# Attention outputs turned in 32x32 blocks by the vector engine instead of as whole tiles by the tensor engine

## The reference

```
q = heads([ctx, LN(x)] @ Wq)                      # 32 heads of 16
k, v = heads(LN(x) @ Wk), heads(LN(x) @ Wv)       # 8 heads, each for 4 query heads
sk, sv = heads(ctx @ Wsk), heads(ctx @ Wsv)
s = q @ [sk, k].T / 4 + slope[head] * (key - query), only where 0 <= query - key < 64
x1 = x + tanh(g0) * (softmax(s) @ [sv, v]) @ Wo
p = softmax(LN(x1) @ w_router); the 4 best of 128 experts, normalised
basis = silu(LN(x1) @ w_gate) * (LN(x1) @ w_up)   # 8 blocks of 256
out = x1 + tanh(g1) * ((sum of blocks by the experts' mix) @ w_down + shared expert)
```

## Time and profile before

| | |
|---|---|
| median of 3 runs | 991.57 us (988.68 to 991.63) |
| the profiled execution | 991.21 us, of which the span is 989.4 |
| PE busy | 923.0 us, 93% of the span |
| DVE busy | 569.0 us, 58% |
| ACT busy | 420.1 us, 42% |
| POOL busy | 370.4 us, 37% |
| mean granted PE clock | 0.984 of full speed |

### The profile page before, as it was taken

How to read it: one execution, slowest core, us unless ns; L and a number is a source line. 1 busy time by engine, 2 the same in 40 slices (tenths; PEclk the granted TensorE clock), 3 DMA queues, 4 the chain that set the end, 5 groups by cost and what they waited for, 6 DMA issues and landing times.

```text
span 989.4 us, 18083 instructions
## 1 busy us (share of the span) xinstructions
PE 923.0 (93%) x6936; PEld 793.9 (80%) x6936; DVE 569.0 (58%) x1135; ACT 420.1 (42%) x906; POOL 370.4 (37%) x401
## 2 busy tenths in 40 slices
PE   6779999999999999989998987899999999999998
PEld 6678989888898989977786775578888888888886
DVE  5356574756657474765122665836565565655657
ACT  5665453454444444464311432334444444344431
POOL 2020010100000010002000998445687887888841
PEclk9979999999999999999999998999999999999999
DMA  6585556665656555698000004461201201201026
GB/s 221 169 204 155 126 157 176 152 183 135 175 142 173 129 152 139 157 250 255 2 21 22 22 22 138 129 219 30 84 27 59 85 22 65 86 22 64 22 91 251
DMA packets 79559, 117.04 MB, mean 118 GB/s; under 512 B 6249, under 2 KB 49002, under 8 KB 78442
## 3 DMA queue, kind: packets, MB, share of 16 engines
q1 hardware_dynamic: 77744, 115.18, 41.0%
q10 hardware_dynamic: 1730, 0.71, 0.3%
HBM read 77.13 MB, written 37.81 MB: 116 GB/s over the span
## 4 chain that ended last, share of the span: by engine, by line
PE 78%; DVE 7%; POOL 5%; DMA 4%; issue 3%; ACT 2%; SPq 1%; ACTq 0%; DVEq 0%; POOLq 0%
PE ps_proj L1521 20%; PE ps_scores L1845 18%; PE ps_scoresT L1845 9%; PE ps_o L1634 5%; PE ps_scoresT L1621 5%; PE ps_proj L1845 4%; PE ps_scores L1600 4%; PE ps_scores L1521 3%; PE ps_o_max L1645 2%; PE ps_scoresT L1521 2%; DMA q_stack<-max_rows 2%; DVE neg_max L1179 1%; PE ps_proj L1544 1%; POOL sum_lo L706 1%; DMA q_kept<-qT_hi 1%
## 5 line engine op out<-in xcount | busy, mean ns | idle before, releaser
L1179 DVE TENSOR_REDUCE neg_max<-ps_scores 128x2 f32<-128x384 f32 (+1 forms) x256 | 130.3, 517 | 127.9 <-PE ps_scores L1600 126.8
L868 ACT ACTIVATE probsT<-ps_scoresT 128x512 f32<-128x512 f32 (+1 forms) x256 | 138.7, 543 | 142.2 <-PE ps_scoresT L1621 139.0
L1070 ACT ACTIVATE part_sums<-ps_scores 128x512 f32<-128x512 f32 x96 | 57.4, 598 | 136.2 <-PE ps_scores L1845 136.2
L1600 PE MATMUL ps_scores<-k_stack,q_stack 114*128 114x192 f32 (+1 forms) x512 | 103.5, 287 | 10.2 <-DVE neg_max L1179 7.4
L1621 PE MATMUL ps_scoresT<-q_stack,k_stack 116*128 116x256 f32 x448 | 104.0, 303 | 5.3 <-DMA q_stack<-max_rows 4.2
L1600 PEld LDWEIGHTS ps_scores<-k_stack,q_stack 114*128 114x128 f32 x512 | 80.2, 193 | 17.6 <-DVE neg_max L1179 11.2
L651 POOL TENSOR_SCALAR var_eps<-mean_var 128x2 f32<-128x2 f32 x8 | 2.1, 260 | 222.0 <-DVE mean_var L1128 221.9
L766 POOL TENSOR_TENSOR big<-big,basis 128x512 f32<-128x512 f32 x56 | 77.5, 1402 | 15.2 <-DVE basis L1471 15.2
L754 POOL TENSOR_TENSOR w_expert_lo<-w_sums,w_expert_hi 128x256 fp32r<-128x256 f32 x64 | 64.3, 1016 | 45.2 <-ACT w_expert_hi L1002 45.2
L1621 PEld LDWEIGHTS ps_scoresT<-q_stack,k_stack 116*128 116x128 f32 x448 | 71.5, 194 | 7.1 <-DMA q_stack<-max_rows 4.7
L1521 PE MATMUL ps_proj<-actT_hi,wq_hi 128*128 128x256 f32 x224 | 65.6, 293 | 0.0
(11 more groups left out here) (264 smaller groups left out, 2561.1 us busy)
## 6 DMA issues: line engine op xcount, KB each, us to landing
k_stack<-k_kept SPq DMA_DIRECT2D x64, 192.0 KB, 5.2
q_stack<-q_kept SPq DMA_DIRECT2D x31, 384.0 KB, 5.3
q_kept<-qT_hi SPq DMA_DIRECT2D x16, 512.0 KB
big<-coeff_rows SPq DMA_DIRECT2D x8, 1024.0 KB, 4.8
xn_rows<-in_x SPq DMA_DIRECT2D x8, 512.0 KB, 4.2
k_kept<-kT_hi SPq DMA_DIRECT2D x16, 256.0 KB
q_kept<-qT_lo SPq DMA_DIRECT2D x8, 512.0 KB
x_rows<-in_x SPq DMA_DIRECT2D x8, 512.0 KB, 5.3
```

The lines of the kernel that those rows point to most:

```text
L868: act.activation(PT[:, g % 2, 2 * j:2 * j + blocks].rearrange("p h f r w -> p (h f r w)"), ST[:, n % 2, 0:blocks].rearrange("p h n -> p (h ...
L1070: act.activation(TP[:, u % 2, j, :], src[:, u % 2, :], ACT.Copy).then_inc(taken, 1)
L1179: dve.tensor_reduce(NM[:, g % 2, 2 * i:2 * i + 2], SA[:, n % 2, :, 0:keys], AX.X, ALU.max, negate=True).then_inc(max_done, 1)
L1600: ins = pe.matmul(SA[:, n % 2, f, 0:2 * (near.stop - near.start)], QS[0:TOP, g, i, f].rearrange("p r w -> p (r w)"), keys[:, near, :].rear ...
```

## The change

- `ps_o` is no longer copied and turned by PE. DVE turns it in one instruction, as 4x8 blocks of 32x32 (`o_turn`, slot 20, behind that slot's `maxima`). Each block is 32 tokens by (16 outputs, 16 equal sums) of one head. DVE takes the reciprocals; POOL multiplies (`scale_outputs`) into half of a buffer for two groups.
- When the second group of a pair is there, DVE turns the buffer back (`o_back_turn`, slot 22 of that group). The result has two groups' outputs as rows of 128 features, one quarter of the contraction of Wo. ACT copies the high half (`o_high`), POOL makes the low half (`o_low`), both in slot 23. The rows of Wo are put in the matching order on the host.
- `pv_out`, `turn_o`, `norm`, `turn_rows`, `rows_high` and `rows_low` go, with their jobs in `projections()` and the wait of `turn_max` for `norm`.
- Both row normalisations in the loop move from DVE to POOL, directly behind the roots.
- `max_halves` stands before the slot's `maxima`, not behind it.
- The turned x1 rows have buffers of their own (`XS`); the low half is stored in two DMAs, not one.
- Offsets: statistics -46, -45; queries -24, -22, -19, -16; values -7, -5; turn of V 15; Wo 52, 55; x1 roots 57; turn of x1 62, 63; the last router product one slot earlier. The query store (`KEEP_Q`, two slots behind the last query product) moves with them.

The diff, cut to its core:

```diff
-NM_TURN, PV, PV_OUT, TURN_O, NORM = 6, LAG + 5, LAG + 6, LAG + 9, LAG + 10
-TURNS_BETWEEN = (TURN_O - NM_TURN) // NB
-LOAD_ROWS, STATS, NORMALISE = -59, (-48, -47), (-38, -37)
-PREP, K_PROJ, Q_PROJ, V_PROJ = (-32, -31, -30, -29), (-27, -26), (-24, -22, -20, -18), (-4, -3)
+NM_TURN, PV, O_TURN, O_BACK, O_HIGH = 6, LAG + 5, LAG + 6, LAG + 8, LAG + 9
+LOAD_ROWS, STATS = -59, (-46, -45)
+PREP, K_PROJ, Q_PROJ, V_PROJ = (-32, -31, -30, -29), (-27, -26), (-24, -22, -19, -16), (-7, -5)
-TURN_V, TURN_ROWS, TIMES_WO, TURN_X = 16, (53, 54), (56, 58), (63, 64)
-LOAD_X1, X1_ROOTS, X1_NORMALISE, KEEP_X = 42, 59, (62, 63), 67
+TURN_V, TIMES_WO, TURN_X = 15, (52, 55), (62, 63)
+LOAD_X1, X1_ROOTS, KEEP_X = 42, 57, 66
...
-ROUTER_AT = {0: 0, 4: 1, 12: 2, 34: 3}
+ROUTER_AT = {0: 0, 4: 1, 12: 2, 33: 3}
...
+    OB = at("o_blocks", 192 * KIB, [P, 2, T // 32, 2 * D])
+    ON = at("o_normal", 194 * KIB, [P, 2, T // 32, 2 * D])
+    OR = [at(f"oT_raw{i}", where, [P, T]) for i, where in enumerate((196 * KIB, 214 * KIB + 256))]
+    XS = {"hi": at("xs_hi", 216 * KIB, [P, HC, T], F32R), "lo": at("xs_lo", 208 * KIB, [P, TB, HC, P], F32R)}
...
+                sp.dma_start(xT_kept_d[b, 0].rearrange("p c n -> p (c n)"),
+                             XS["hi"][:].rearrange("p c n -> p (c n)").bitcast(F32)).then_inc(xT_kept, 16)
+                for t in range(TB):
+                    sp.dma_start(xT_kept_d[b, 1][:, :, t * P:(t + 1) * P], XS["lo"][:, t].bitcast(F32)).then_inc(xT_kept, 16)
...
+        def scale_outputs(n):
+            p, odd = divmod(n, 2)
+            pool.wait_ge(inv_done, n + 1)
+            if odd == 0 and p >= 2:
+                pool.wait_ge(o_back, p - 1)
+            pool.tensor_tensor(ON[:, p % 2, :, odd * D:(odd + 1) * D], OB[:, n % 2, :, 0:D],
+                               RI[:, n % 2].unsqueeze(2).broadcast_to([P, T // 32, D]), ALU.mult).then_inc(o_done, 1)
+
+        def o_low(p):
+            c = p % HC
+            pool.wait_ge(oT_hi, p + 1)
+            pool.tensor_tensor(OT["lo"][:, :, c, :], OR[p % 2][:].rearrange("p (t n) -> p t n", t=TB),
+                               OT["hi"][:, :, c, :].bitcast(F32), ALU.subtract).then_inc(oT_lo, 1)
+
+        def normalise(b):
+            for t in range(TB):
+                n = b * TB + t
+                pool.wait_ge(rstd_done, b + 1)
+                pool.tensor_scalar(XN[:, t, :], XN[:, t, :], mv[:, n, 0:1], rstd[:, n:n + 1],
+                                   ALU.subtract, ALU.mult).then_inc(xn_done, 1)
...
+        def o_high(p):
+            b, c = divmod(p, HC)
+            act.wait_ge(o_back, p + 1)
+            if c == 0 and b >= 1:
+                act.wait_ge(wo_mm, TB * b)
+            act.activation(OT["hi"][:, :, c, :], OR[p % 2][:].rearrange("p (t n) -> p t n", t=TB), ACT.Copy
+                           ).then_inc(oT_hi, 1)
...
-        def norm(n):
-            b, g = divmod(n, HK)
-            dve.wait_ge(o_turned, n + 1)
-            v = PN.rearrange("p (t r e) -> p t r e", t=TB, r=G)
-            dve.reciprocal(RI[:], v[:, :, :, D]).then_inc(inv_done, 1)
...
+        def o_turn(n):
+            dve.wait_ge(pv_mm, n + 1)
+            if n >= 2:
+                dve.wait_ge(o_done, n - 1)
+            dve.transpose(OB[:, n % 2].rearrange("p k e -> p (k e)"), PO).then_inc(o_turned, 1)
+            dve.wait_ge(o_turned, n + 1)
+            dve.reciprocal(RI[:, n % 2], OB[:, n % 2, :, D]).then_inc(inv_done, 1)
+
+        def o_back_turn(p):
+            dve.wait_ge(o_done, 2 * (p + 1))
+            if p >= 2:
+                dve.wait_ge(oT_lo, p - 1)
+            dve.transpose(OR[p % 2][:], ON[:, p % 2].rearrange("p k e -> p (k e)")).then_inc(o_back, 1)
...
         def times_wo(b, t):
             dst = take_bank("wo", b, t)
-            pe.wait_ge(pj_done, passed("rows", b, t))
+            pe.wait_ge(oT_lo, HC * (b + 1))
             product(dst, lambda h, c: OT[h][:, t, c, :], lambda h, c: WO[h][:, c, :], range(HC)).then_inc(wo_mm, 1)
```

More of the change, by code:

```diff
@@ L226, in build @@
     gates, tg = little("gates", [P, 2]), little("tanh_gates", [P, 2])
-    RI = little("inv_sums", [P, TB, G])
+    RI = little("inv_sums", [P, 2, T // 32])
     amp, amp2, mix = little("amp", [P, KB, 2]), little("amp2", [P, KB]), little("mix", [P, KB])
@@ L664, in x1_roots, with x1_normalise @@
             inverse_roots(x1_mv, x1_ve, x1_rstd, x1_tmp, b).then_inc(x1_rt, 1)
+        def scale_outputs(n):
[16 more added lines that the diff above has]
+                                   ALU.subtract, ALU.mult).then_inc(xn_done, 1)
+        def x1_normalise(b):
+            if b >= 1:
+                pool.wait_ge(xT_mm, TB * b)
+            if 1 <= b <= SPILLED:
+                pool.wait_ge(xT_kept, 48 * b)
+            for t in range(TB):
+                n = b * TB + t
+                pool.wait_ge(x1_rt, b + 1)
+                pool.tensor_scalar(X1N[:, t, :], X1[:, t, :], x1_mv[:, n, 0:1], x1_rstd[:, n:n + 1],
+                                   ALU.subtract, ALU.mult).then_inc(x1_n, 1)
         def weights_low(n):
@@ L687, in _ @@
                 x_roots(b)
+                normalise(b)
             b = due(n, X1_ROOTS)
@@ L690, in _ @@
                 x1_roots(b)
+                x1_normalise(b)
+            m = group_due(n, O_TURN)
+            if m is not None:
+                scale_outputs(m)
+            m = group_due(n, O_HIGH)
+            if m is not None and m % 2:
+                o_low(m // 2)
             s = n - (END - UNITS)
@@ L948, in _ @@
             for t in range(TB):
-                b = due(n, TURN_ROWS[t] + 1)
-                if b is not None:
-                    rows_high(b, t)
                 b = due(n, TURN_X[t] + 1)
@@ L971, in _ @@
                 act.activation(tg[:], gates[:], ACT.Tanh).then_inc(tg_done, 1)
-            m = group_due(n, PV_OUT)
-            if m is not None:
-                pv_out(m)
+            m = group_due(n, O_HIGH)
+            if m is not None and m % 2:
+                o_high(m // 2)
             s = n - (END - UNITS)
             if s == 18:
-                split_hi(0)
+                split_hi(0, (xT_kept, 48 * SPILLED))
             if s == 20:
@@ L1270, in _ @@
         for n in range(SLOTS):
-            m = group_due(n, NORM)
+            m = group_due(n, NM_TURN - 2)
             if m is not None:
-                norm(m)
+                max_halves(m)
             if n < END:
                 maxima(n)
+            m = group_due(n, O_TURN)
+            if m is not None:
+                o_turn(m)
+            m = group_due(n, O_BACK)
+            if m is not None and m % 2:
+                o_back_turn(m // 2)
             for i in range(4):
@@ L1293, in _ @@
             for t in range(TB):
-                b = due(n, TURN_ROWS[t] + 1)
-                if b is not None:
-                    rows_low(b, t)
                 b = due(n, TIMES_WO[t] + 1)
@@ L1732, in _ @@
                 times_v(m)
-            m = group_due(n, TURN_O)
-            if m is not None:
-                turn_o(m)
             for i in range(4):
@@ L1758, in _ @@
                 turn_v(b)
-            for t in range(TB):
-                b = due(n, TURN_ROWS[t])
-                if b is not None:
-                    turn_rows(b, t)
             for t in range(TB):
@@ L1935 @@
     arrays, aps = {}, {}
+    heads = inputs["L0_xattn_Wo"].reshape(HK // 2, 2, G, D, HID)
+    inputs["L0_xattn_Wo"] = np.asarray(heads).transpose(0, 2, 1, 3, 4).reshape(HID, HID)
     for name, v in {**inputs, **constants()}.items():
```

77 lines of the change are left out of this document (11 added, 66 removed).

## The result

The changed kernel takes 983.12 us (median of 7 runs, 977.94 to 984.65), the kernel before 991.63 beside it (7 runs, 988.68 to 997.66): a ratio of 0.989, 95% interval 0.985 to 0.992. It is faster, by 8.5 us between the medians and 12 us between the two profiled executions (979.26 us after, of which the span is 977.4), where 28 were forecast. 983 lies outside the range of 948 to 978. The profiled execution of the changed kernel is one of its two fastest, so tables by stage show more gain than the medians.

What follows compares the result with a forecast made beforehand. PE was taken to bound most of each batch, DVE an 11.6 us stretch. Five batches at 3.6 us gave 18.0; with 1.5, 3.7, 1.0 and 3.8 elsewhere, 28.0 us gained: 963.2 us (963.5 from the median), range 948 to 978.

Steps and rivals of the forecast that it cites:

- turn pairs: PE's two transposes per group of output sums, 0.37 us of chain each group: removing them gains 2.6 us a batch.
- row turns: PE's eight output-row transposes per batch, 0.49 + 0.44 us of chain: removing them gains 0.9 us a batch.
- statistics: Row statistics moved from slots 16 and 17 to 18 and 19, norm no longer ahead of the maxima: 0.6 us gained a batch.
- Wo's wait and residual: Ahead of Wo, PE waits for the last pair's turn back, copy and split: about 0.4 us lost a batch.
- DVE's total: DVE's work per batch: loses 5.9 us, gains twelve transposes of 4.9 us, so falls by 1.0 us.
- rival C: DVE and POOL block each other on SBUF, stretching the maxima's low halves: 1 us a batch, 970 us; chance 0.12.
- POOL's normalisation: Row normalisations of 512 elements moved to POOL, 1.0 us each, four per batch; POOL stays no bound.
- The last batch: Last key products to first router product: 4.7 us gained, though PE work saved before the 431 to 440 us transfer buys nothing.
- rival D: DVE's transpose of four-byte data is slow; at 1.6 us each it costs 38 us: 1001 us; chance 0.06.
- B: Q store and stack load land late, PE stands in slot 0 of each batch: 12 us, 975 us; chance 0.09.
- Rival A: The 11.6 us DVE-paced stretch shrinks too, by 1.5 us a batch, 9 us over six: 954 us; chance 0.13.
- E: PE's turns were covered: PE idles instead and DVE's or ACT's pace returns half: 977 us; chance 0.08.

Runs made afterwards that it cites:

- e1: The changed kernel with 64 unread pairs of PE transposes put back directly behind P times V: 989.61 us, ratio 0.994.
- h1: The changed kernel with Wo one slot later, plus unread PE transposes for the eight row turns per batch, in slots 17 and 19: 981.35 us, 0.986.
- g3: The changed kernel with Wo one slot later and only the x1 normalisation back on DVE: 981.11 us, 0.986.
- e4: The changed kernel with both row normalisations of the loop back on DVE: 982.85 us, 0.988.
- h2: The changed kernel with Wo one slot later and the row statistics back at their old offsets (-48, -47): 1017.5 us, 1.023.
- e8: The changed kernel with the maxima's halves behind the slot's maximum, as before: 988.64 us, 0.994.
- e3: The changed kernel with the value products back in slots 28 and 29: 995.34 us, 1.000.
- e6: The changed kernel with Wo in slots 53 and 56 and the x1 roots in slot 58, one later each: 974.98 us, 0.982.
- g1: The same kernel as e6, with Wo and x1 roots one slot later than in the changed kernel, measured again: 974.16 us, 0.979.
- e5: The kernel before with only the new offsets of statistics, queries, values and the turn of V: 1004.59 us, 1.012.

## Why the prediction was wrong

The direction was right: PE lost its turns and the time fell. The sizes were wrong. By the terms of the sum, per middle batch:

| step | forecast | measured by itself | run |
|---|---|---|---|
| turn pairs | +2.6 | +1.2 | `e1` |
| row turns | +0.9 | +0.4 (in slots 17 and 19) | `h1` |
| x1's normalisation off DVE | +1.0 | +0.7 (both norms: +0.5) | `g3`, `e4` |
| statistics | +0.6 | no gain; 8.4 lost where they stood | `h2` |
| halves ahead | 0 | +0.7 | `e8` |
| block turns where DVE sets the pace | -0.6 | not by itself; the stretch is 0.3 us shorter | trace |
| value products | -0.5 | +0.7 | `e3` |
| Wo's wait and residual | -0.4 | -1.3 | `e6`, `g1` |
| sum | +3.6 | +1.55 for the whole change | |

The single prices don't add up to the whole, since each was taken with all the others in place, and `e5` shows how far they hang together (-2.1 for four of the offsets in the old kernel).

**The failed step** is "A group's two transposes cost 0.37 us of chain", and the 0.93 for the rows with it. Both were read from the chain and booked in full. `e1` shows 0.15 us for a pair, `h1` 0.43 for the rows. Two faults are in it. For the pairs, the piece of the chain holds about 0.19 us that falls to whoever comes behind P times V (I had noted that the 270 ns of one matmul is no price since matmuls overlap; the pieces have a like fault). For the rows, the piece was the price between close products, but in `h1` DVE's pace covers nearly half of it. Of the 3.6 us of the sum, 3.5 hung on these turns; with the 1.6 measured it comes to 1.7. That this is close to 1.55 is partly luck, since the other terms, 0.1 in sum as forecast, were singly off by -0.9 to +1.2 and happen to cancel. For the pairs the profile of before had a view that shows it: PE's timeline, by starts and not by ends.

```profile
77.48 0.97 PE L1634 MATMUL ps_o<-probsT,v_ones 128*32 128x128 f32 x32
78.38 0.44 PE L1645 MATMUL ps_o_max<-ident,oT_sums 128*128 128x128 f32 x2
78.57 0.42 PE L1600 MATMUL ps_scores<-k_stack,q_stack 114*128 114x128 f32 x2
```

The turns start at 78.38 and the scores behind them at 78.57: 0.19 us for the pair. Starts do not show what is covered: by them the rows of a middle batch are 0.73 (235.57 to 235.95, 236.61 to 236.96).

**DVE's total** did not fall by 1.0 us a batch; it is 35.15 both times. The products and splits that left, 5.9 us, and the transposes that came, 5.2 (3.5 + 1.7), were sized well, within 0.3. The rest is the mechanism of rival C, at 1.0 us of DVE a batch: a pair of halves takes 0.45 us in the mean instead of 0.33. DVE and POOL at 254.5 us in the changed kernel:

```profile
254.50 0.14 DVE L1222 CAST max_halves<-neg_max 128x8 fp32r<-128x8 f32 x1
254.68 0.59 DVE L1224 TENSOR_TENSOR max_halves<-neg_max,max_halves 128x8 fp32r<-128x8 f32 x1
```

```profile
254.49 0.75 POOL L678 TENSOR_TENSOR oT_lo<-oT_raw,oT_hi 128x256 fp32r<-128x256 f32 x1 [3.52 <-ACT oT_hi L918]
```

The low half of 8 elements ends at 255.27, as POOL's subtraction does (255.24). SBUF — State Buffer of the Trainium skill, "Who interferes with whom", has a DVE instruction with two SBUF inputs contend with a POOL one that reads SBUF, and the trace agrees. Rival C had the mechanism and 1 us a batch. That this microsecond of DVE costs the batch time is not shown: `e8` is without it and longer, for the order of its halves.

**POOL's normalisation** was put at 1.0 and takes 2.08 us. The nearest rows were two-input products of 512 elements, 1.29 us, and I took them for an upper bound; a form with two scalars per row, read from memory, is no relative of them. The GPSIMD Engine Reference of the Trainium skill, section 3.1, gives 769 ns for a 512-element loop, as its best case; the measurement is 2.7 times that. Its cost in this kernel is indirect: 6.4 us of roots and rows in POOL's order, which begin 0.56 us behind the low half that Wo waits for (`h2` shows the price where they begin ahead of it). "In POOL's queue the scalings behind it wait" was right in kind; I had not followed the low half ahead of Wo.

**The last batch** was to gain 4.7 us and lost 1.1. I had said that PE work saved ahead of a transfer buys nothing, and applied it to 431 to 440 us alone. After, the waits for DVE and the gaps without a releaser are longer there, and some 10 us for 3.4 run at the low clock, which eats most of the PE work saved. Why the gap and the clock differ is open. The forecast had no term for any of the three.

**What held.** DVE's transposes, so rival D is out; no late query stack (B), PE waits for none in a middle batch; a wait on oT_lo ahead of Wo of 0.5 us for 0.4. The tail gained 3.8 of 3.8: rows (0.87) and x_normal with Wo earlier as forecast, but six pairs at `e1`'s price are 0.9 and not 1.5, so a part of the agreement is luck. The start's 1.35 for 1.5 is within the scatter. Rival A did not occur: from the scores of slot 30 to the mark the DVE stretch takes 11.5 us (245.43 to 256.90) for 11.8 (195.28 to 207.09), 0.3 less where A had 1.5. By my own sign, "wrong if the batch stays above 54 us", it was wrong at 54.25. E, that the turns were covered, gave the nearest time (977), and holds in part: the rows were half covered where `h1` puts them, the pairs were mostly cheap.

## What to carry to other kernels

Price an instruction in a full pipeline by what the next one's start moves, not by its piece of the chain, and check the sum of such prices against a second view (starts in the timeline, or the follower's piece where the instruction is missing). Then ask which engine is next in line there: what it covers is not won. When work moves to an idle engine, follow that engine's order for every short instruction behind the long one, and find the one for which the bound engine waits. Then move each wait that is left by one slot: here that was worth 7 to 10 us by the ratios (0.982 and 0.979 for 0.989), about as much as the change.

## What the hardware showed that was not expected

- The first PE piece behind the 32 small products of P times V takes about 0.19 us more in the chain (0.37 for 0.18 to 0.20), for turns and for scores.
- A POOL `tensor_scalar` with two per-row scalars of 128x512 takes 2.08 us; POOL's product of two tensors of this size takes 1.29.
- A DVE subtraction of 8 elements a row with both inputs in SBUF takes 167 ns alone and up to 1215 ns; where it is long it ends with POOL's instruction (255.27 and 255.24, 458.65 and 458.62).
- DVE's block transpose of 128x256 four-byte values takes 431 to 451 ns out of PSUM and 430 to 446 in SBUF, close to a reduction (421) or a subtraction (414) of that size.
- The granted clock was 0.50, the level of 1.2 GHz, for 5.5 us behind a PE wait of 5.5 us (`h2`) and for 6.6 us behind one of 1.5 (`e3`): Wo took 5.46 us for 2.99, P times V 1.65 for 0.90. In each batch this cost 2.9 and 3.0 us of busy time (53.82 for 50.91, 53.98 for 50.98). The same 1.5 us wait left the clock at 1.00 in the first batches of `e3`.
- Of the gaps of PE without a releaser in the last stretch, up to 5.4 us long, ten of seventeen ended within 0.5 us of the start of an 8 KB "instruction" transfer.
